# The head attentions of a vision tower leave the row statistics to the norms behind them

## The chip, the cores and the metric

One core of a Trainium2 chip runs the whole program. The time is that of one execution on the device, in microseconds; of several executions the median is given. Beside it there is one profiled execution, whose trace gives the start and length of each instruction.

## The reference

A small vision tower on 32 images of 50 tokens (49 patches and a class token), 192 features, float32. Four layers follow the patch embedding, each a mixer and a feed-forward part, each behind a layer norm and added to h. What matters here lies in layers 1 and 2:

```python
# layer 1's feed-forward part: a transformer block with experts, on x = layernorm(h)
#   LN(ln1) -> attention of 12 heads of 16 -> projection, added -> LN(ln2) -> 8 experts, top 2
h = h + _L1_ffn_ref(_layernorm(h), ...)
# layer 2's mixer: attention of 12 heads with q and k of length one
h = h + _L2_attn_ref(_layernorm(h), ...)
# layer 2's feed-forward part: 8 experts with a capacity, on the norm of what the mixer wrote
h = h + _L2_ffn_ref(_layernorm(h), ...)
```

A layer norm takes mean and variance over the 192 features of each token.

## The kernel before

The 1600 tokens lie as 16 tiles of 100 tokens (two images), a token to a partition, in h and x (100 x 16 x 192). Each stage is a block with one program for each engine; between two blocks there is a barrier of all engines. Semaphores order the engines within a block.

`heads_attention` (line 1378) is used twice: in layer 1 it adds to x, and GpSimd adds each finished tile of x to h (`join`, line 1428); in layer 2 it adds to h, and there is no join. Its loop runs over the tiles, two to a round of the hardware loop. In a step VectorE copies the transposed queries and keys of the next tile out of PSUM (`take_qkT`, lines 1646 and 1647), adds the output projection of the last tile to its row (`add`, 1662), takes the highest scores (1651), scales q and k into `wide` (1638, or 1633 in layer 2), multiplies by the inverse sums (1656), copies v (1642), and at the end of the step takes the statistics of the tile that it added (`count`, 1667, a bn_stats into t.bn). TensorE transposes q and k (1465), multiplies the scores (1479, 1487), weighs the values (1496), projects the output (1504) and makes the q, k, v of a later tile (1453, 1454). After the loop VectorE counts the last tile and turns the 16 sets of statistics into mean and variance in t.mv (bn_aggr, 1707).

`normalise` (line 286) is the norm in front of every part. It goes in four groups of four tiles. For a group `collect` takes the statistics (bn_stats 353, bn_aggr 356), unless `ready` says that t.mv holds them, and adds eps (366); ScalarE takes the root (408) behind a table load (403); `spread` takes the reciprocal (371). VectorE does collect(g) ahead of spread(g - 1). Then the rows are scaled (324), some by VectorE in spread, the others by GpSimd, which waits for a group's reciprocal. TensorE transposes each pair of tiles (453), and ScalarE copies them into xT (415, or 418 in two instructions with gain and bias). Who scales a tile is set by these lines:

```python
turn = [2 if ready or i >= TILES - GROUP else GROUP if y is None else TILES for i in range(TILES)]
by_vector = [i for i in range(TILES) if i % turn[i] == 0 and turn[i] < TILES]
```

The norm of layer 2's mixer (line 2150) comes behind experts, loads its h from memory and takes its own statistics. The norm of the last layer's experts (line 2543) does so too. Behind the norm of an expert part comes the router's block, with a table load (1118) and matmuls of the gate (1111).

Of the kernel before, what the change touches and what calls it, by code (L numbers as in the profile page):

```python
# [24 lines left out]
TILES = TOKENS // TILE  # L25
# [1127 lines left out]
def turn(t, src, dst):  # L1153

    nc = t.nc
    n = src.shape[2]
    turned = t.sem("turned")
    with t.block() as block:
        @block.tensor
        def _(pe):  # L1160
            for i in range(TILES):
                nc.tensor.transpose(t.bank[i // 4][0:n, TILE * (i % 4):TILE * (i % 4 + 1)], src[:, i, :],
                                    t.w["ident"][0:TILE, 0:TILE]).then_inc(turned, 1)

        @block.scalar
        def _(act):
            for c in range(CHUNKS):
                act.wait_ge(turned, 4 * c + 4)
                nc.scalar.activation(dst[:, CHUNK * c:CHUNK * (c + 1)], t.bank[c][0:n, 0:CHUNK], ACT.Identity)
# [208 lines left out]
def heads_attention(t, wqkv, proj, dst, unit, total=None):  # L1378
# [5 lines left out]
    nc, w = t.nc, t.w  # L1384
    GROUPS, DEEP = HEADS // 4, HEAD + 3
    with ExitStack() as st:
# [15 lines left out]
        (cleared, wproj_in, biased, staged, projected, values_up, squared, summed, logged, rooted, q_done, v_done,  # L1402
         turned, qkT_done, scored, max_done, shift_turned, shiftedT_done, scoredT, exp_done, weighed, sums_logged,
         inv_done, a_done, out_done, added, front_step) = (t.sem(n) for n in names)
        counted = t.sem("counted")
        bankQ, bankV, bankO, bankR, bankS = t.bank[0], t.bank[1], t.bank[2], t.bank[3], t.bank[4:8]
        wholeS = t.psum[0:TILE, 4 * 512:8 * 512].rearrange("p (j n) -> p j n", j=4)[:, :, 0:GROUPS * TILE]
        kT_at = slice(DIM, DIM + GROUPS * TILE)
# [1 line left out]
        with t.block() as block:  # L1410
# [194 lines left out]
            def _(dve):  # L1605
# [12 lines left out]
                def lengths(n):  # L1618
                    if unit:
                        dve.wait_ge(squared, n + 1)  # L1620
                        nc.vector.tensor_reduce(norm[:, 2, :], sq[:].rearrange("p (h e) -> p h e", e=HEAD),
                                                AX.X, ALU.add).then_inc(front_step, 1)
                        dve.wait_ge(front_step, 2 * n + 1)

                        nc.vector.tensor_scalar(norm[:, 0, :], norm[:, 2, :], 1e-24, None, ALU.max).then_inc(summed, 1)

                def take_qk(n, v):
                    if unit:
                        dve.wait_ge(rooted, n + 1)
                        nc.vector.tensor_tensor(norm[:, 1, 0:HEADS], norm[:, 1, 0:HEADS], w["L2_scale"][:],  # L1630
                                                ALU.mult).then_inc(front_step, 1)
                        dve.wait_ge(front_step, 2 * n + 2)
                        nc.vector.tensor_tensor(wide[:, v, :, 0:HEAD], narrow,
                                                norm[:, 1, :].unsqueeze(2).to_broadcast([TILE, 2 * HEADS, HEAD]),
                                                ALU.mult).then_inc(q_done, 1)
                    else:
                        dve.wait_ge(projected, n + 1)
                        nc.vector.tensor_scalar(wide[:, v, :, 0:HEAD], narrow, HEAD ** -0.25, None, ALU.mult).then_inc(q_done, 1)

                def take_v(n, v):  # L1640
                    dve.wait_ge(values_up, n + 1)
                    nc.vector.tensor_copy(v_[:, v, :, 0:HEAD], bankV[0:TILE, 0:DIM].rearrange("p (h e) -> p h e", e=HEAD)).then_inc(v_done, 1)

                def take_qkT(n):
                    dve.wait_ge(turned, n + 1)
                    nc.vector.tensor_copy(qkT[:, 0], bankQ[:, 0:GROUPS * TILE].rearrange("p (g n) -> p g n", g=GROUPS))
                    nc.vector.tensor_copy(qkT[:, 1], bankV[:, kT_at].rearrange("p (g n) -> p g n", g=GROUPS)).then_inc(qkT_done, 1)

                def highest(n, v):
                    dve.wait_ge(scored, n + 1)  # L1650
                    nc.vector.tensor_reduce(wide[:, v, 0:HEADS, HEAD + 2].rearrange("p (g j) -> p j g", j=4),
                                            wholeS.rearrange("p j (g n) -> p j g n", g=GROUPS), AX.X, ALU.max).then_inc(max_done, 1)

                def weighted(n):
                    dve.wait_ge(inv_done, n + 1)
                    nc.vector.tensor_tensor(aT[:].rearrange("p g n -> p (g n)"), bankO[:, 0:GROUPS * TILE],
                                            inv[:].rearrange("p g n -> p (g n)"), ALU.mult).then_inc(a_done, 1)

                def add(n):
                    dve.wait_ge(out_done, n + 1)  # L1660
                    tile = dst[:, bass.ds(n, 1), :]
                    nc.vector.tensor_tensor(tile, tile, bankO[0:TILE, 0:DIM].unsqueeze(1), ALU.add).then_inc(added, 1)

                def count(n):
                    dve.wait_ge(added, n + 1)
                    at = bass.ds(n, 1)
                    nc.vector.bn_stats(t.bn[:, at, :], dst[:, at, :]).then_inc(counted, 1)

                def step(n, u, first=False, final=False):
                    if not final:  # L1670
                        take_qkT(n + 1)
                    if not first:
                        add(n - 1)
                    if not final:
                        highest(n + 1, 1 - u)
                        if unit:
                            lengths(n + 2)
                            take_qk(n + 2, u)
                            weighted(n)
                        else:  # L1680
                            weighted(n)
                            take_qk(n + 2, u)
                        take_v(n + 2, u)
                    else:
                        weighted(n)
                    if not first:
                        count(n - 1)

                lengths(0)
                take_qk(0, 0)  # L1690
# [5 lines left out]
                take_v(1, 1)  # L1696
                dve.wait_ge(biased, 1)
                step(0, 0, first=True)
                with dve.Fori(0, TILES // 2 - 1) as i:
                    for u in range(2):  # L1700
                        step(2 * i + u + 1, 1 - u)
                step(TILES - 1, 1, final=True)
                add(TILES - 1)
                count(TILES - 1)
                for i in range(TILES):
                    dve.wait_ge(counted, i + 1)
                    nc.vector.bn_aggr(t.mv[:, i, :], t.bn[:, i, :])

BLOCK = 256
SUBS = BLOCK // 128  # L1710
# [414 lines left out]
def gates(t, w, rows):  # L2125
    return [w[0:rows, 0, :], w[0:HALF, 1, :]]


def xT_tile(t, rows):
    return lambda i, k: t.xT[0:rows if k == 0 else HALF, k, TILE * i:TILE * (i + 1)]  # L2130


def layer1_ffn(t):

    w = t.w
    normalise(t, t.h, 1e-5, keep=t.x, second=1e-5, gain=w["L1_ln1_g"], bias=w["L1_ln1_b"], ready=True)
    heads_attention(t, w["L1_qkv"], "L1_proj", t.x, unit=False, total=t.h)
    normalise(t, t.x, 1e-5, keep=t.x, gain=w["L1_ln2_g"], bias=w["L1_ln2_b"], ready=True)
    with ExitStack() as st:
        share = t.sbuf("share8", [TILE, TILES, 8], st)  # L2140
        shareT = t.sbuf("shareT", [8, 1, TOKENS], st)
        picked = [t.sbuf(f"pick{j}", [TILE, TILES, 8], st) for j in range(2)]
        route(t, xT_tile(t, HALF + 1), gates(t, w["L1_gate"], HALF + 1), 8, 2, masks=picked, weights=share)
        turn(t, share, shareT[:, 0, :])
        add_back(t, shareT, t.h, lambda g, i: w["L1_b2"][:, g, :])
        experts(t, "L1", t.x, t.h, picked, share, 8, ACT.Gelu, gated=False, norm=w["L1_ln2"])


def layer2_mixer(t):
    normalise(t, t.h, 1e-5, load=t.sums)  # L2150
    heads_attention(t, t.w["L2_qkv"], "L2_proj", t.h, unit=True)
# [6 lines left out]
def layer2_ffn(t):  # L2158


    nc, w = t.nc, t.w
    E, M = L2_EXPERTS, HIDDEN // 128
    size = [TILE, TILES, E]
    normalise(t, t.h, 1e-5, keep=t.x, ready=True)
    with ExitStack() as st:
        combine = t.sbuf("combine", [128, E // 2, TOKENS], st)
        taken = t.sbuf("taken", [HALF, 2, E, GROUPS2, SLOTS2], st)
# [383 lines left out]
def tower(nc, args, out, where):  # L2551
    with ExitStack() as stack:
        t = Tower(nc, stack, args, where)
        embed(t)
        zero_spare(t)
        layer0_mixer(t)
        layer0_ffn(t)
        layer1_mixer(t)
        layer1_ffn(t)
        layer2_mixer(t)  # L2560
        layer2_ffn(t)
        layer3_mixer(t)
        layer3_ffn(t, out)
# [190 lines left out]
```

## Time and profile before

| | |
|---|---|
| time, median of 3 executions | 2697.13 us (2692.56 to 2702.44) |
| time of the profiled execution | 2709.01 us |
| its span, first to last instruction | 2707.1 us |
| its mean granted TensorE clock | 0.847 |
| TensorE matmuls busy | 2114.3 us, 78% |
| VectorE busy | 1240.3 us, 46% |
| ScalarE busy | 858.6 us, 32% |
| GpSimd busy | 838.9 us, 31% |

The busy shares are means over stages with different limits. The span leaves out what lies around the first and last instruction (1.9 us here). The granted clock is given as a part of 2.4 GHz: 1.00 is that, 0.50 is 1.2 GHz. Layer 1's head attention and the norm behind it lie between about 647 and 798 us of the span, layer 2's between about 1052 and 1220 us.

### The profile page before, as it was taken

The page shows a single profiled execution, that of the slowest core. Times are in us where ns is not written, and L with a number is a line of the kernel's source. Part 1 is how long each engine was busy: PE and PEld are TensorE (multiplying, and loading weights), DVE is VectorE, ACT ScalarE, POOL GpSimd, SP SyncE. Part 2 cuts the span into 40 slices and gives each one's busy share as a digit, 9 for nine tenths or more (in the row PEclk, how much of TensorE's full clock was granted, in tenths as well). Part 3 has the DMA queues.
Part 4 walks back from the last instruction along what each step waited for, and adds up shares of the span by engine and source line. Part 5 has one row for each costly group of instructions (what it writes and reads, how often), then busy time and mean ns, then how long its engine had stood idle before and what let it go on. Part 6 is the DMA issues. An engine that isn't in the chain of part 4 may idle for free. (4 is left out here: it accounts for less than half of the span.)

```text
span 2707.1 us, 41933 instructions
## 1 busy us (share of the span) xinstructions
PE 2114.3 (78%) x13260; PEld 1508.9 (56%) x13260; DVE 1240.3 (46%) x2831; ACT 858.6 (32%) x1713; POOL 838.9 (31%) x788
## 2 busy tenths in 40 slices
PE   9746778886985894986899737777489944999998
PEld 9412224574763783654467312222479933999987
DVE  4249992323544113553113479998622236222222
ACT  1247862122332332342111545554112212111111
POOL 0204542203121553010001247665134421434443
PEclk9658996775876995997899769999689966999999
DMA  7000000000004761000210000000267614777774
GB/s 214 15 0 1 0 0 0 0 0 7 0 1 118 204 180 31 0 0 0 70 52 18 0 0 0 0 0 0 53 204 221 198 24 142 228 223 229 217 203 126
DMA packets 77951, 201.86 MB, mean 75 GB/s; under 512 B 17777, under 2 KB 47348, under 8 KB 69524
## 3 DMA queue, kind: packets, MB, share of 16 engines
q1 hardware_dynamic: 52820, 169.74, 19.6%
q0 software_dynamic: 25056, 31.22, 6.7%
q8 instruction: 35, 0.57, 0.1%
q14 instruction: 40, 0.33, 0.0%
HBM read 179.25 MB, written 22.91 MB: 75 GB/s over the span
## 5 line engine op out<-in xcount | busy, mean ns | idle before, releaser
L1858 POOL DMA_INDIRECT sums<-yblock,put x129 | 205.8, 1596 | 422.1 <-DVE yblock L2121 245.5
L1906 PE MATMUL banks<-xTblock,wt 128*128 128x256 f32 (+1 forms) x1464 | 268.0, 340 | 1.6 <-ACT xTblock L1977 1.2
L1931 PE MATMUL banks<-wt,hid 128*128 128x192 f32 x1548 | 267.2, 327 | 0.0
L2111 DVE TENSOR_TENSOR hid<-sa,banks 128x512 f32<-128x512 f32 (+1 forms) x183 | 105.8, 578 | 339.3 <-ACT sa L1998 336.4
L1931 PEld LDWEIGHTS banks<-wt,hid 128*128 128x128 f32 x1548 | 251.5, 191 | 0.1
L1906 PEld LDWEIGHTS banks<-xTblock,wt 128*128 128x128 f32 x1464 | 237.1, 194 | 23.5 <-issue 1.6
L1998 ACT ACTIVATE sa<-banks 128x512 f32<-128x512 f32 (+1 forms) x183 | 93.3, 510 | 481.6 <-PE banks L1917 476.6
L722 PE MATMUL banks<-g,consts 128*128 128x400 f32 x384 | 184.7, 571 | 60.2 <-DVE g L861 56.2
L830 POOL TENSOR_TENSOR w<-u,spreadB 128x400 f32<-128x400 f32 x192 | 192.7, 1033 | 87.2 <-ACT spreadB L801 87.2
L1853 POOL DMA_INDIRECT xblock<-table,take x135 | 135.0, 1000 | 223.3 <-DVE put L2087 175.3
L855 DVE TENSOR_TENSOR_SCAN s<-banks,w 128x400 f32<-128x400 f32 x192 | 188.9, 984 | 4.2 <-POOL w L830 4.2
L324 POOL TENSOR_SCALAR rows<-h,mv,sd 100x192 f32<-100x192 f32 x69 | 69.9, 1026 | 328.0 <-DVE sd L371 328.0
L722 PEld LDWEIGHTS banks<-g,consts 128*128 128x128 f32 x384 | 61.0, 197 | 168.5 <-DVE g L861 167.2
L613 POOL TENSOR_TENSOR w<-u,r 128x400 f32<-128x400 f32 x96 | 99.1, 1034 | 175.4 <-ACT r L587 162.9
L785 ACT ACTIVATE banks<-rate,coef 128x392 f32 x192 | 113.2, 591 | 117.8 <-DVE s L855 117.8
L2121 DVE TENSOR_SCALAR yblock<-banks,gate 128x192 f32<-128x192 f32 x129 | 49.4, 415 | 208.3 <-PE banks L1931 208.3
L1917 PE MATMUL banks<-xTblock,wt 64*128 64x256 f32 (+1 forms) x1464 | 143.2, 342 | 0.0
L1917 PEld LDWEIGHTS banks<-xTblock,wt 64*128 64x128 f32 x1464 | 116.0, 187 | 22.9 <-issue 11.9
L861 DVE TENSOR_TENSOR g<-s,banks 128x400 f32<-128x400 f32 x192 | 104.7, 547 | 0.0
L2304 PE MATMUL banks<-taken,wu 96*128 x192 | 86.3, 610 | 12.7 <-DMA wd<-L_down 10.0
L636 DVE TENSOR_TENSOR_SCAN s<-banks,w 128x400 f32<-128x400 f32 x96 | 94.3, 983 | 0.1
L453 PE MATMUL banks<-consts,rows 100*96 100x100 f32 (+1 forms) x192 | 44.3, 368 | 61.5 <-DVE rows L324 35.8
(416 smaller groups left out, 3743.5 us busy)
## 6 DMA issues: line engine op xcount, KB each, us to landing
wt<-L3f_packed SPq DMA_DIRECT2D x41, 1152.0 KB, 5.8
wt<-L3f_packed SPq DMA_DIRECT2D x41, 576.0 KB, 6.0
wt<-L3m_packed SPq DMA_DIRECT2D x20, 1152.0 KB, 5.7
wt<-L_packed SPq DMA_DIRECT2D x20, 579.0 KB, 4.4
wt<-L3m_packed SPq DMA_DIRECT2D x20, 577.0 KB, 5.9
wt<-L_packed SPq DMA_DIRECT2D x20, 576.0 KB, 4.2
pixels<-pixels SPq DMA_DIRECT2D x16, 375.0 KB, 5.0
wu<-L_up SPq DMA_DIRECT2D x8, 576.0 KB, 4.7
```

What stands on the lines that cost most here:

```text
L613: nc.gpsimd.tensor_tensor(w1[:, j % SLOTS, :], u[:, group(j), at], r[:, j % SLOTS, :], ALU.mult).then_inc(w1_done, 1)
L722: nc.tensor.matmul(acc[g][0:parts, 0:CHUNK], ident[0:parts, 0:parts], g_[:, j % SLOTS, :], start=(n == 0), stop=(n == STATES - 1)).then_in ...
L785: nc.scalar.activation(rest, rate[:, g, at].rearrange("p (b t) -> p b t", t=SEQ)[:, :, 1:SEQ], ACT.Exp, scale=coef[:, g, n:n + 1]).then_in ...
L830: nc.gpsimd.tensor_tensor(w2[:, j % SLOTS, :], u[:, g, at], spreadB[:, n % 2, :], ALU.mult).then_inc(bu_done, 1)
L855: nc.vector.tensor_tensor_scan(s[:, j % SLOTS, :], decays[j % DECAYS], w2[:, j % SLOTS, :], 0.0, ALU.mult, ALU.add).then_inc(s_done, 1)
L861: nc.vector.tensor_tensor(g_[:, j % SLOTS, :], s[:, j % SLOTS, :], bankC[(j // groups) % 2][0:parts, 0:CHUNK], ALU.mult).then_inc(g_done, 1)
L1853: nc.gpsimd.indirect_dma_start(x[:, b % 2, q - column_of_block[b], :], None, table, bass.IndirectOffsetOnAxis(take[:, q:q + 1], 0)).then_i ...
L1858: nc.gpsimd.indirect_dma_start(t.sums, bass.IndirectOffsetOnAxis(put[:, q:q + 1], 0), y[:, b % 2, q - column_of_block[b], :], None, comput ...
L1906: nc.tensor.matmul(bank[:, n * j:n * (j + 1)], wt[:, v, cols(base, 2 * p + j)], xT[:, v, 0, 0:n], start=(j == 0), stop=False, skip_group_c ...
L1917: last = nc.tensor.matmul(bank[:, n * j:n * (j + 1)], wt[half, v, cols(REST_AT, 2 * p + j)], xT[half, v, 1, 0:n], start=False, stop=True, ...
L1931: last = nc.tensor.matmul(bankY[s], hid[:, m, 128 * s:128 * (s + 1)], wt[:, v, DOWN_AT + DIM * m:DOWN_AT + DIM * (m + 1)], start=(m == 0 a ...
L2111: nc.vector.tensor_tensor(hid[:, 2 * p:2 * p + 2, 0:n], sa[:, (PAIRS * v + p) % 2, 0:2 * n].rearrange("p (m n) -> p m n", m=2), second[:, ...
```

## The change

The head attention no longer takes statistics of the rows that it writes, in the loop or behind it, and the semaphore `counted` goes. The two norms behind it (lines 2138 and 2164) are called without `ready`, so that they take bn_stats and bn_aggr in their own groups, and the list `turn` comes out as for the other norms without `ready`.

```diff
@@ heads_attention
-        counted = t.sem("counted")
...
-                def count(n):
-                    dve.wait_ge(added, n + 1)
-                    at = bass.ds(n, 1)
-                    nc.vector.bn_stats(t.bn[:, at, :], dst[:, at, :]).then_inc(counted, 1)
-
                 def step(n, u, first=False, final=False):
...
                     else:
                         weighted(n)
-                    if not first:
-                        count(n - 1)
...
                 step(TILES - 1, 1, final=True)
                 add(TILES - 1)
-                count(TILES - 1)
-                for i in range(TILES):
-                    dve.wait_ge(counted, i + 1)
-                    nc.vector.bn_aggr(t.mv[:, i, :], t.bn[:, i, :])
@@ layer1_ffn
-    normalise(t, t.x, 1e-5, keep=t.x, gain=w["L1_ln2_g"], bias=w["L1_ln2_b"], ready=True)
+    normalise(t, t.x, 1e-5, keep=t.x, gain=w["L1_ln2_g"], bias=w["L1_ln2_b"])
@@ layer2_ffn
-    normalise(t, t.h, 1e-5, keep=t.x, ready=True)
+    normalise(t, t.h, 1e-5, keep=t.x)
```

## Rows read from the trace of the kernel before

**Rows 1.** The page's first line: span and instructions.

```profile
span 2707.1 us, 41933 instructions
```

**Rows 2.** Timeline, layer 1's loop, high clock: start, us, engine, line, operation [idle before].

```profile
730.12 0.35 DVE L1667 BATCH_NORM_STATS2 bn<-x  x1
...
736.86 0.35 DVE L1667 BATCH_NORM_STATS2 bn<-x  x1
...
737.97 0.47 DVE L1646 COPY qkT<-banks 128x300 f32<-128x300 f32 x1 [0.76 <-PE banks L1465]
```

**Rows 3.** The removed line's own view: durations in ns, and who waited.

```profile
L1667 DVE BATCH_NORM_STATS2 bn<-x x16: 349/350/360, 687.6 to 783.8; - x14, 100x6 f32<-100x192 f32 x2
...
who waited for it (us, times):
busy tenths in 40 slices 0000000000000000000000000000000000000000
```

**Rows 4.** Timeline, layer 2's loop, high clock.

```profile
1192.05 0.35 DVE L1667 BATCH_NORM_STATS2 bn<-h  x1
...
1193.47 0.47 DVE L1646 COPY qkT<-banks 128x300 f32<-128x300 f32 x1 [1.07 <-PE banks L1465]
```

**Rows 5.** Timeline, layer 1's loop at the low clock.

```profile
674.93 0.36 DVE L1642 COPY v<-banks 100x192 f32<-100x192 f32 x1 [1.22 <-PE banks L1454]
...
687.33 0.36 DVE L1642 COPY v<-banks 100x192 f32<-100x192 f32 x1 [1.22 <-PE banks L1454]
...
689.79 0.47 DVE L1646 COPY qkT<-banks 128x300 f32<-128x300 f32 x1 [1.83 <-PE banks L1465]
```

**Rows 6.** Timeline, the seam from layer 1's attention to the router.

```profile
783.45 0.35 DVE L1662 TENSOR_TENSOR x<-x,banks 100x192 f32<-100x192 f32 x1 [1.04 <-PE banks L1504]
...
783.88 0.59 POOL L1428 TENSOR_TENSOR h<-h,x 100x192 f32<-100x192 f32 x1 [3.92 <-DVE x L1662]
784.12 1.15 DVE L1707 BATCH_NORM_AGGREGATE mv<-bn 100x2 f32<-100x6 f32 x16
...
785.57 0.24 DVE L366 TENSOR_SCALAR sd<-mv 100x4 f32<-100x4 f32 x2 [0.31 <-PEq L104]
...
787.35 8.39 POOL L324 TENSOR_SCALAR x<-x,mv,sd 100x192 f32<-100x192 f32 x8 [2.87 <-DVE sd L371]
...
797.59 1.28 ACT L1118 ACT_TABLE_LOAD   x1 [0.27 <-PEq L104]
```

**Rows 7.** Timeline, the seam from layer 2's attention to the router.

```profile
1206.45 0.35 DVE L1662 TENSOR_TENSOR h<-h,banks 100x192 f32<-100x192 f32 x1 [1.04 <-PE banks L1504]
...
1207.12 1.15 DVE L1707 BATCH_NORM_AGGREGATE mv<-bn 100x2 f32<-100x6 f32 x16
...
1208.57 0.24 DVE L366 TENSOR_SCALAR sd<-mv 100x4 f32<-100x4 f32 x2 [0.30 <-PEq L104]
...
1220.12 1.28 ACT L1118 ACT_TABLE_LOAD   x1 [0.27 <-PEq L104]
```

**Rows 8.** Timeline, the norms of lines 2150 and 2543, with their successors' first instructions.

```profile
1036.17 1.14 DVE L353 BATCH_NORM_STATS2 bn<-h 100x6 f32<-100x192 f32 x4 [15.39 <-DMA h<-sums]
...
1039.51 11.10 POOL L324 TENSOR_SCALAR rows<-h,mv,sd 100x192 f32<-100x192 f32 x11 [14.49 <-DVE sd L371]
...
1052.03 1.28 ACT L1561 ACT_TABLE_LOAD   x1 [0.27 <-PEq L104]
...
2195.03 1.14 DVE L353 BATCH_NORM_STATS2 bn<-h 100x6 f32<-100x192 f32 x4 [15.59 <-DMA h<-sums]
...
2211.28 1.28 ACT L1118 ACT_TABLE_LOAD   x1 [0.27 <-PEq L104]
```

**Rows 9.** Timeline of GpSimd, first instruction behind a block that GpSimd ended.

```profile
647.17 1.38 POOL L1418 MEMSET wide<- 100x1536 f32 x1 [0.29 <-POOLq L104]
```

**Rows 10.** Windows behind the seams: stretch, us, TensorE busy, granted clock, DMA share, GB/s.

```profile
784.00:866.00 82.00, 41.39 (x191) 0.50 0.26 73
1208.00:1248.00 40.00, 25.23 (x120) 0.50 0.00 1
1248.00:1300.00 52.00, 38.35 (x125) 0.89 0.00 0
```

## What the change does to the time: the prediction

> **What bounds the kernel here.** I read the page first, then the timeline of both attentions at either clock, then the line of the removed statistics for who waits for it, then the two seams from attention to norm, then a norm of this kernel that already takes its own statistics, and last the granted clock behind the seams. The profiled execution has a span of 2707.1 us [rows 1] and a time of 2709.01 us; the three other executions have a median of 2697.13 us (2692.56 to 2702.44), so the profiled one was 0.4% slower than that. No single engine bounds the whole: the program is a row of stages with a barrier between each two, and a microsecond counts in a stage only if it lies on what that stage ends with. So the change touches four stages: two attentions, two norms. A measurement of this kernel can tell about 0.3%, 8.1 us, from no change.
>
> Inside the attention loops the statistics are the last thing VectorE does in a tile. In the first attention at the high clock (2.4 GHz) they start at 730.12 and again at 736.86, so a tile takes 6.74 us; they end at 737.21, and the copy of qkT behind them starts at 737.97 after 0.76 us of idling, released by TensorE's transposes [rows 2]. In the second attention the idle time behind them is 1.07 us [rows 4]. At the low clock (1.2 GHz) a tile takes 687.33 - 674.93 = 12.40 us, and VectorE idles 1.83 us there [rows 5]. The list of those who wait for the statistics is empty: the line of the heading is followed at once by the next heading's line [rows 3].
>
> **The change, part by part.**
>
> *The statistics in the loops (32 of 0.35 us), price 0.* What hides them is the wait for TensorE that follows. Without them the copy of qkT waits 0.35 us longer for the same transposes, which go by score_turned and v_done and not by the statistics. What would be bought if that cover weren't there is 32 x 0.35 = 11.2 us; this is the bound from below for the term. I take 0, since the idle time behind them (0.76 us at the least) is more than the pitch of 0.35 us. Above nothing there is nothing: no wait is added in the loops, and GpSimd's order there is untouched.
>
> *The end of the attentions.* In the first one the last add ends at 783.45 + 0.35 = 783.80; then come the statistics of the last tile and the 16 aggregations, which end at 784.12 + 1.15 = 785.27, and VectorE starts the norm at 785.57, 0.30 later. With the tail gone, GpSimd's last addition of x to h is what ends the block: 783.88 + 0.59 = 784.47 [rows 6]. Another block that GpSimd ended was followed 0.29 later by its successor [rows 9], so the norm starts at 784.77: 0.80 us saved. In the second attention GpSimd has no such addition, the last add ends at 1206.45 + 0.35 = 1206.80, the norm can start 0.30 later at 1207.10 and not at 1208.57 [rows 7]: 1.47 us saved. The count of tile 14, in the last step, lies in a wait for TensorE too and saves nothing. Together -2.27 us, the surest term.
>
> *The norms themselves.* Dropping `ready=True` does two things. The first is plain: collect(g) now runs four bn_stats and four bn_aggr before the variance, and since collect(1) stands ahead of spread(0) on VectorE, GpSimd's first tile waits for two groups of statistics. The second stands in the list `turn`: with ready every second tile is VectorE's (8 and 8); without it, and without y, every fourth is, and every second only in the last four, so VectorE has tiles 0, 4, 8, 12, 14 and GpSimd the eleven others. GpSimd's tiles follow each other without a gap, 8.39 us for 8 [rows 6], and it is their pace that the transposes, ScalarE's copies and the end of the norm go by.
>
> The price of both is in the trace already, since the norm behind the first experts (line 2150) is this very form: no second, no y, keep apart, 5 and 11 tiles. Its first statistics start at 1036.17, GpSimd starts 3.34 us later at 1039.51 and takes 11.10 us for its eleven, and the next block starts at 1052.03: 15.86 us from the first statistics to the successor. A second norm of the form took 2211.28 - 2195.03 = 16.25 us, a little of it a wait for its loads [rows 8]. The norms that are changed took 797.59 - 785.57 = 12.02 us [rows 6] and 1220.12 - 1208.57 = 11.55 us [rows 7] from VectorE's first instruction to the successor. The second has the same tail behind GpSimd as the form of rows 8, so it costs 15.86 - 11.55 = +4.31. The first has gain and bias, so that its last pair is copied in two instructions: behind GpSimd's end at 787.35 + 8.39 = 795.74 it takes 1.85 us. So it comes to 3.34 + 11.10 + 1.85 = 16.29, less 12.02 = +4.27. The bounds: below, if GpSimd kept eight tiles, only the later start counts, 3.34 less (787.35 - 785.57 = 1.78) = +1.56 for each; above, 16.25 for the form of rows 8, 0.39 us more for each. I take +4.31 and +4.27, by the nearest row. Square roots are no new term: ScalarE's table load lies beside the statistics, while before it was what VectorE waited for. Nothing runs beside these blocks that would hide the eleven tiles: TensorE and ScalarE wait for each, and no DMA is issued in them.
>
> The Trainium skill, SBUF — State Buffer (Who interferes with whom), has a rule that speaks of this move: VectorE and GpSimd share a port pair, and one blocks the other while it holds it, but an instruction of VectorE with at most one SBUF input outside the two-port modes does not contend. bn_stats has one input, so by the page the moved statistics cost GpSimd nothing; were they blocked for GpSimd's time, up to twelve bn_stats of 0.35 us, 4.2 us, would come on top for each norm. The trace agrees with the page: eleven tiles with statistics beside them took 11.10 us, 1.01 us each, and eight without took 8.39 us, 1.05 us each [rows 6, 8].
>
> *What follows.* Routing and experts start behind a barrier and issue their own loads, so they are moved and not changed. One semaphore less in each attention is one clearing less on SyncE, off the path. The sum: -2.27 + 4.27 + 4.31 = **+6.3 us**. On the profiled time that is 2715.3 us, on the median of the runs 2697.13 + 6.3 = 2703.4 us, 0.23% more.
>
> **The clock.** Behind both seams TensorE's granted clock is 0.50 (1.2 GHz) already: 784 to 866, and 1208 to 1248 [rows 10]. It fell when the attention's matmuls ended, so a norm that is 4 us longer has none to lose. What can move is where it rises again, and in the stretch 1248 to 1300 it goes up and down, 0.89 in the mean: (1 - 0.89) / 0.50 = 0.22 of 52 us, 11.4 us, at the low level, in which a stage that TensorE bounds could give back half or lose as much again: 5.7 us. This is chance from execution to execution, and I take 0 for it; four executions of the kernel before lie between 2692.56 and 2709.01 us.
>
> **The rivals.**
>
> *A: the clock moves with the norms.* The norms' 4 us of sparse transposes make the rise of the clock come later at one or two places behind. For it: the clock rose only at 866 behind the first and at 1248 behind the second, after stretches where TensorE worked 41.39 of 82 and 25.23 of 40 us. Against it: these stages start behind barriers and do the same work in the same order. Price, one stretch as above: +5.7, which gives 2709.1 us. The Trainium skill, TensorE: Matmul & The Clock Gate (Part 1), says that the throttled level is the default and that activity lifts it; by that rule more quiet time can only hurt, and the rows show the low level on both sides of the seam, so it has nothing to hurt inside the norm.
>
> *B: the same phase works the other way*, and the stretch of 0.89 comes out at the high clock: 6.3 - 5.7 = +0.6, 2697.7 us. For and against as with A.
>
> *C, the other side: the statistics in the loop were not hidden.* If TensorE's transposes are themselves let go by something behind the bn_stats on VectorE, each tile becomes 0.35 us shorter, 11.2 us in all, and with 6.3 the sum is -4.9: 2692.2 us. It decides from 6.3 / 32 = 0.20 us a tile on. For it: only that VectorE has the statistics inside each tile's round. Against it: nobody waits for them, and 0.76 us or more of idling comes right behind [rows 2 to 5].
>
> *D: the split stays 8 and 8* (or GpSimd's pace isn't what ends the norm): 1.56 x 2 - 2.27 = +0.9, 2698.0 us. The code of `turn` and rows 8 speak against it.
>
> **The chances.** Forecast 0.72, A 0.12, B 0.08, C 0.05, D 0.03. The median of a few executions moves by some 4 us either way, so of the forecast's 0.72 about 0.24 lie above 8.1 us, and of A most: slower 0.36; faster needs C and luck: 0.03; within 0.3%: 0.61. The range of the likeliest case alone is 2699 to 2708. With A, B and D in it and that scatter it is 2695 to 2711, which leaves out C and the far end of A, under 2 in 10.
>
> **What the profile after would show.** The tile rounds unchanged, 6.74 us in the first attention at the high clock, with the idle time ahead of the qkT copy grown to about 1.1 us. The norms' first bn_stats 0.3 us behind GpSimd's last addition in the first seam and behind VectorE's last add in the second. GpSimd's scaling 11 tiles in each norm, starting 3.3 us behind the first statistics. 16.3 and 15.9 us from there to the router's block. Clock 0.50 through both norms. The prediction is wrong if a tile round shrinks (C), if the norms have 8 tiles on GpSimd (D), or if the stages behind them change their length at another clock (A, B).

## The result, and the profile after

| | kernel before | changed kernel |
|---|---|---|
| median of 22 executions each | 2700.31 us | 2709.65 us |
| ratio | | 1.0035, 95% interval 1.0019 to 1.005 |
| a second comparison, 12 executions of the changed one | 2701.65 us | 2708.36 us, 1.0027, 1.0009 to 1.0045 |
| span of the profiled execution | 2707.1 us | 2702.2 us |

The change makes the kernel slower, by 0.27 and 0.35% in the two comparisons. The forecast was 2703.4 us and 0.23% more. (One of the 22 executions of before, 2850 us, was disturbed, and the ratios leave it out.)

The profiled execution of the changed kernel is 4.9 us *shorter* than that of before. Whoever compares the two spans gets the wrong sign. The changed kernel's profile was already 3.75 us ahead when the first attention concerned began (643.42 against 647.17), before anything that was changed; what the stages behind that point add is in the table. The stages are cut at ScalarE's table loads, of which each begins a block: 403 begins a norm, 1561 (1560 in the changed kernel) a head attention, 1118 the router.

| stage, us | before | changed | changed, second profile |
|---|---|---|---|
| layer 1's attention | 138.36 | 132.31 | 137.64 |
| the norm behind it | 12.06 | 16.47 | 16.49 |
| layer 2's attention | 156.50 | 154.65 | 150.57 |
| the norm behind it | 11.59 | 15.98 | 16.04 |

The norms come out the same in both profiles; the attentions don't. They are read below at their tails and rounds, at one level of TensorE's clock. (Layer 2's attention is the least steady stage of all: 150.57 us here in the second profile of the change, and 164.77 in that of experiment 6, which has the attention of before.)

The first seam in the changed kernel, timeline of all engines, which answers to [rows 6]:

```profile
774.42 0.35 DVE L1661 TENSOR_TENSOR x<-x,banks 100x192 f32<-100x192 f32 x1 [1.31 <-PE banks L1503]
774.85 0.59 POOL L1427 TENSOR_TENSOR h<-h,x 100x192 f32<-100x192 f32 x1 [3.92 <-DVE x L1661]
775.73 1.28 ACT L403 ACT_TABLE_LOAD   x1 [3.13 <-PEq L104]
775.77 1.14 DVE L353 BATCH_NORM_STATS2 bn<-x 100x6 f32<-100x192 f32 x4 [1.00 <-PEq L104]
...
777.22 0.17 DVE L366 TENSOR_SCALAR sd<-mv 100x4 f32<-100x4 f32 x1
777.30 1.13 DVE L353 BATCH_NORM_STATS2 bn<-x 100x6 f32<-100x192 f32 x4
...
778.82 0.17 DVE L371 RECIPROCAL sd<-sd 100x4 f32<-100x4 f32 x1
...
779.10 11.26 POOL L324 TENSOR_SCALAR x<-x,mv,sd 100x192 f32<-100x192 f32 x11 [3.66 <-DVE sd L371]
...
792.20 1.28 ACT L1118 ACT_TABLE_LOAD   x1 [0.27 <-PEq L104]
```

The reader is to see two things. GpSimd's last addition ends at 775.44 and the norm's first statistics start 0.33 later; from the last add's end (774.77) it is 1.00 us, where it was 785.57 - 783.80 = 1.77. And the first reciprocal stands behind two groups of statistics, so that GpSimd starts 3.33 us into the norm (before: 1.78) with eleven tiles in 11.26 us (before: eight in 8.39).

The second seam, VectorE's timeline; behind it GpSimd's and ScalarE's of the same stretch:

```profile
1201.79 0.35 DVE L1661 TENSOR_TENSOR h<-h,banks 100x192 f32<-100x192 f32 x1 [1.31 <-PE banks L1503]
1202.47 1.14 DVE L353 BATCH_NORM_STATS2 bn<-h 100x6 f32<-100x192 f32 x4 [0.32 <-PEq L104]
```

```profile
1205.79 11.19 POOL L324 TENSOR_SCALAR x<-h,mv,sd 100x192 f32<-100x192 f32 x11 [27.09 <-DVE sd L371]
```

```profile
1202.43 1.28 ACT L403 ACT_TABLE_LOAD   x1 [2.45 <-PEq L104]
...
1218.41 1.28 ACT L1118 ACT_TABLE_LOAD   x1 [0.27 <-PEq L104]
```

Here nothing of GpSimd's stands in the seam, and the norm starts 0.33 us behind the last add's end at 1202.14; it was 1.77 [rows 7].

The two norms by engine, windows of the changed kernel and then of before (us, busy time of PE, PEld, DVE, ACT and POOL with their instructions, granted clock, DMA share, GB/s):

```profile
775.73:792.20 16.47, 8.13 (x32) 4.17 (x32) 8.40 (x45) 9.21 (x21) 11.26 (x11) 0.50 0.00 0
1202.43:1218.41 15.98, 8.12 (x32) 4.16 (x32) 8.36 (x45) 5.88 (x14) 11.19 (x11) 0.50 0.00 1
```

```profile
785.53:797.59 12.06, 7.45 (x32) 4.45 (x32) 4.27 (x16) 9.23 (x22) 8.39 (x8) 0.50 0.00 1
1208.53:1220.12 11.59, 7.45 (x32) 4.45 (x32) 4.18 (x16) 5.88 (x13) 8.35 (x8) 0.50 0.00 1
```

VectorE's work doubles, from 4.3 to 8.4 us, and is still well under the norm's length; GpSimd is the busiest engine in both norms of the changed kernel. Before it was so in layer 2's alone: in layer 1's ScalarE was busy 9.23 us (1.28 of it the table load) and GpSimd 8.39. The clock is 0.50 in all four.

The loop of layer 1, VectorE's timeline of the changed kernel, answers to [rows 2]:

```profile
700.58 0.36 DVE L1641 COPY v<-banks 100x192 f32<-100x192 f32 x1 [0.36 <-PE banks L1453]
701.96 0.47 DVE L1645 COPY qkT<-banks 128x300 f32<-128x300 f32 x1 [1.03 <-PE banks L1464]
...
708.71 0.47 DVE L1645 COPY qkT<-banks 128x300 f32<-128x300 f32 x1 [1.03 <-PE banks L1464]
```

A tile takes 708.71 - 701.96 = 6.75 us with the statistics gone, as it did with them. The idle time ahead of the copy went from 0.76 to 1.03 us: what was removed became waiting. In layer 2 it went from 1.07 to 1.34, with rounds of 7.98 us in both kernels.

The whole of layer 1's attention says the same, if profiles are paired in which the clock rose at the same point. The first row is the changed kernel's; the two behind it are of experiment 1, which keeps the statistics in the loop:

```profile
643.42 1.28 ACT L1560 ACT_TABLE_LOAD   x1 [6.61 <-PEq L104]
```

```profile
642.84 1.28 ACT L1561 ACT_TABLE_LOAD   x1 [6.64 <-PEq L104]
...
773.83 0.35 DVE L1662 TENSOR_TENSOR x<-x,banks 100x192 f32<-100x192 f32 x1 [1.04 <-PE banks L1504]
```

From this load to the last add's end it is 774.77 - 643.42 = 131.35 us without the statistics and 774.18 - 642.84 = 131.34 with them. Where the clock rose later it is 136.67 without (second profile of the change) and 136.63 with (783.80 - 647.17, the kernel before).

By these stages the change costs 4.41 + 4.39 in the norms less 0.77 + 1.44 in the tails: **+6.6 us**, 0.24%, inside both measured intervals.

### The profile page after: what moved, and what is told of

The parts are those of the page before. It is cut to its first block and busy times, and to the rows that moved or that the text cites. A ratio compares the mean times of both kernels' runs of the same rounds, so it can differ in the third digit from the quotient of the medians.

```text
span 2702.2 us, 41903 instructions
## 1 busy us (share of the span) xinstructions
PE 2104.1 (78%) x13260; PEld 1500.7 (56%) x13260; DVE 1237.1 (46%) x2825; ACT 857.5 (32%) x1713; POOL 844.0 (31%) x794
```

## The experiments

Whole times scatter from one execution to the next (2691 to 2711 us for the kernel before), by more than these edits are worth, so each is read first at its stages, and the ratio stands beside it where it was timed.

**1. The norms alone.** The attentions stay as before; the norms lose `ready`, and the statistics are taken twice.

```diff
-    normalise(t, t.x, 1e-5, keep=t.x, gain=w["L1_ln2_g"], bias=w["L1_ln2_b"], ready=True)
+    normalise(t, t.x, 1e-5, keep=t.x, gain=w["L1_ln2_g"], bias=w["L1_ln2_b"])
...
-    normalise(t, t.h, 1e-5, keep=t.x, ready=True)
+    normalise(t, t.h, 1e-5, keep=t.x)
```

> The attentions stay as before, statistics and aggregations included; only the two norms lose ready, so that they take the statistics a second time. My theory: the whole loss is in the norms, the gain in the tails of the attentions. So the two norms take 16.4 and 16.0 us from table load to table load, against 12.06 and 11.59 before, the tails stay at 1.77 us from the last add's end to the norm, and the sum is +8.8 us, about 2.2 more than the change has by its stages. Rival (the loss of the change is partly elsewhere, for example in the attentions' loops without statistics): this kernel would then be nearer to before than the change is, under +6 us.

Measured: norms of 16.48 and 15.97 us, tails unchanged (last add's end to the norm 1.76 us both times), so +8.8 by the stages; ratio 1.0046, interval 1.0027 to 1.0064, that is +12.4 us (7.3 to 17.3). The whole loss is there with the attentions untouched, and by the stages it is larger than the change's own +6.6, as it should be where the tails save nothing; the ratios alone can't tell the two apart, since their intervals overlap. The rival's "under +6" is outside the interval.

**2. Eight tiles each.** The changed kernel, but `turn` is 2 for these two norms.

```diff
-    turn = [2 if ready or i >= TILES - GROUP else GROUP if y is None else TILES for i in range(TILES)]
+    turn = [2 if ready or halves or i >= TILES - GROUP else GROUP if y is None else TILES for i in range(TILES)]
```

> The changed kernel, but in the two norms VectorE and GpSimd take eight tiles each, as with ready. My theory, in which GpSimd's eleven tiles are most of the loss and the later start the smaller part: GpSimd still starts 3.3 us behind the first statistics, and works 8.4 us; the norms take about 13.6 and 13.2 us in place of 16.4 and 16.0, and the whole is about 1 us slower than before. Rival (the statistics on VectorE set the pace of the norm, not GpSimd's share): the norms stay within 1 us of 16.4 and 16.0, since VectorE has three more tiles of 0.38 us beside its statistics.

Measured: norms of 14.12 and 13.71 us, 2.35 and 2.27 shorter than the changed kernel's; ratio 1.0015 (0.9994 to 1.0037), stages +2.06 + 2.12 - 2.21 = +2.0 us. So just over half of the norms' loss was the split (2.35 of 4.41 and 2.27 of 4.39). They are 0.5 us longer than I expected, and GpSimd's timeline shows why:

```profile
787.15 2.09 POOL L324 TENSOR_SCALAR x<-x,mv,sd 100x192 f32<-100x192 f32 x2 [3.65 <-DVE sd L371]
789.57 2.10 POOL L324 TENSOR_SCALAR x<-x,mv,sd 100x192 f32<-100x192 f32 x2 [0.32 <-DVE sd L371]
791.99 4.07 POOL L324 TENSOR_SCALAR x<-x,mv,sd 100x192 f32<-100x192 f32 x4 [0.32 <-DVE sd L371]
```

With two tiles of a group GpSimd is done before VectorE has the next reciprocal, and it idles 0.32 us twice. The rival is right in that small part: at eight tiles each, VectorE's statistics begin to set the pace.

**3. Scale at once.** The changed kernel, but VectorE does spread(g) right behind collect(g) in these two norms.

```diff
                 for g in range(GROUPS):
                     collect(g)
-                    if g:
+                    if at_once:
+                        spread(g)
+                    elif g:
                         spread(g - 1)
-                spread(GROUPS - 1)
+                if not at_once:
+                    spread(GROUPS - 1)
```

> The changed kernel, but VectorE scales a group and releases it to GpSimd right after that group's own statistics, not after the next group's. My theory (the start is late because two groups of statistics lie ahead of the first reciprocal): GpSimd starts about 2.1 us behind the first statistics in place of 3.3, and each norm is 1.1 to 1.2 us shorter, 15.3 and 14.8 us. Rival (VectorE's wait for ScalarE's root in each group makes VectorE late for later groups, and GpSimd runs dry): gaps between GpSimd's tiles, and the norms no shorter than 16.4 and 16.0.

Measured: norms of 15.08 and 14.66 us, 1.39 and 1.32 shorter. VectorE's timeline, then GpSimd's:

```profile
784.89 1.14 DVE L353 BATCH_NORM_STATS2 bn<-x 100x6 f32<-100x192 f32 x4 [1.00 <-PEq L104]
...
786.78 0.18 DVE L371 RECIPROCAL sd<-sd 100x4 f32<-100x4 f32 x1 [0.27 <-ACT sd L411]
```

```profile
787.06 11.02 POOL L324 TENSOR_SCALAR x<-x,mv,sd 100x192 f32<-100x192 f32 x11 [2.51 <-DVE sd L371]
```

GpSimd starts 2.17 us into the norm and not 3.33, and has no gap in its eleven tiles. The wait for the root costs VectorE 0.27 us there and GpSimd nothing. So the later start is the other part of the loss, as far as it comes from the second group's statistics: 1.16 us of start, and 0.24 in GpSimd's own time (11.02 against 11.26), which I had not expected. This order and the split of experiment 2 were not run together. The whole time of its one execution says nothing at this size.

**4. Four counts.** The kernel before, with each tile's statistics taken four times.

```diff
+        scratch = t.sbuf("scratch", [TILE, 3, 1, 6], st)
...
                     nc.vector.bn_stats(t.bn[:, at, :], dst[:, at, :]).then_inc(counted, 1)
+                    for k in range(3):
+                        nc.vector.bn_stats(scratch[:, k], dst[:, at, :])
```

> The kernel before, but each tile's statistics are taken four times in the attention loops (three go to a scratch tile that nobody reads). It asks how much cover there is. My theory (hidden behind the wait for TensorE's transposes: 0.76 us idle in layer 1, 1.07 in layer 2): three more of 0.27 to 0.35 us take 0.8 to 1.05 us, so a round in layer 1 goes from 6.745 to between 6.75 and 7.05 us and in layer 2 it stays at 7.98. Rival C of the prediction (the statistics are in the tile's round in full): 7.6 to 7.8 us and 8.8 to 9.0 us.

Measured, VectorE's timeline in layer 1 and then in layer 2:

```profile
717.72 0.47 DVE L1647 COPY qkT<-banks 128x300 f32<-128x300 f32 x1
...
723.63 0.86 DVE L1670 BATCH_NORM_STATS2 scratch<-x 100x6 f32 x3
724.47 0.47 DVE L1647 COPY qkT<-banks 128x300 f32<-128x300 f32 x1
...
1172.72 0.47 DVE L1647 COPY qkT<-banks 128x300 f32<-128x300 f32 x1 [0.29 <-PE banks L1466]
...
1180.71 0.47 DVE L1647 COPY qkT<-banks 128x300 f32<-128x300 f32 x1 [0.29 <-PE banks L1466]
```

Rounds of 6.75 and 7.99 us. Three more bn_stats take 0.78 us of VectorE's time (1.07 - 0.29 in layer 2), and the rounds don't grow. In layer 1 the cover is used to its end: no idle time is left ahead of the copy. Rival C is refuted from the costly side, as it was from the cheap one by the changed kernel's own rounds. (The last tile's three stand behind the last add, where nothing covers them: from there to the norm it is 2.54 us in layer 1, 0.77 more than before.)

**5. Early aggregations.** The kernel before, with 14 of the 16 bn_aggr in the last step, behind add(14).

```diff
+                    if final:
+                        aggregate(range(n - 1))
...
                 count(TILES - 1)
-                for i in range(TILES):
-                    dve.wait_ge(counted, i + 1)
-                    nc.vector.bn_aggr(t.mv[:, i, :], t.bn[:, i, :])
+                aggregate((TILES - 2, TILES - 1))
```

> The kernel before with its statistics in the loop, but 14 of the 16 aggregations stand in the last step, ahead of the wait for the last tile's inverse sums, and only two stay behind the last add. My theory (a tail can be had for nothing without moving the statistics): the aggregations lie in idle time of VectorE, the last add ends as before, and the norm starts about 0.95 us behind it in place of 1.77 in both attentions; in layer 1 GpSimd's last addition to h ends first or at the same time. The norms keep 12.06 and 11.59 us. Sum -1.6 us. Rival: the aggregations push the last tile's work and the seam gains nothing.

Measured, the second seam, VectorE's timeline:

```profile
1190.43 0.35 DVE L1662 TENSOR_TENSOR h<-h,banks 100x192 f32<-100x192 f32 x1 [1.56 <-PE banks L1504]
1190.70 1.03 DVE L1672 BATCH_NORM_AGGREGATE mv<-bn 100x2 f32<-100x6 f32 x14
1193.16 0.47 DVE L1656 TENSOR_TENSOR aT<-banks,inv 128x300 f32<-128x300 f32 x1 [1.43 <-ACT inv L1589]
...
1194.94 0.35 DVE L1662 TENSOR_TENSOR h<-h,banks 100x192 f32<-100x192 f32 x1 [1.05 <-PE banks L1504]
...
1195.61 0.30 DVE L1672 BATCH_NORM_AGGREGATE mv<-bn 100x2 f32<-100x6 f32 x2
1196.21 0.24 DVE L366 TENSOR_SCALAR sd<-mv 100x4 f32<-100x4 f32 x2 [0.30 <-PEq L104]
```

The fourteen aggregations lie in VectorE's wait for the inverse sums, and the norm starts 0.92 us behind the last add's end at 1195.29 in place of 1.77; in the first seam 1.00. That is -0.85 and -0.77, with norms of 11.88 and 11.55 us, 0.18 and 0.04 less than before. In layer 1 this is all that the change won at this seam. There GpSimd's addition to h sets the end either way (here at 775.39), so the 0.95 us that I expected in both seams could not be reached.

**6. Three tiles of four on VectorE.** The kernel before, with another split in the two norms.

```diff
-    by_vector = [i for i in range(TILES) if i % turn[i] == 0 and turn[i] < TILES]
+    by_vector = [i for i in range(TILES) if (i % GROUP < 3 if most else i % turn[i] == 0 and turn[i] < TILES)]
```

> The kernel before, but in the two norms VectorE scales three tiles of four and GpSimd one. It tests the same cause from the other side: if GpSimd's share is what a norm's length goes by, fewer tiles on it must shorten the norm until VectorE or ScalarE takes over. My theory: GpSimd works about 4.2 us, layer 1's norm is then set by ScalarE's sixteen copies of 0.46 us and takes 10 to 11 us in place of 12.06, layer 2's by VectorE and takes 8.5 to 9.5 us in place of 11.59; the sum is -3 to -5 us. Rival (the port that VectorE and GpSimd share, or the barrier and table load, set the length): less than 1 us each.

Measured: norms of 10.16 and 8.66 us in place of 12.06 and 11.59, -4.8 us in all; ratio 0.9984 (0.9965 to 1.0003). GpSimd's timeline in the second norm, then ScalarE's of the same stretch:

```profile
1206.10 5.07 POOL L324 TENSOR_SCALAR x<-h,mv,sd 100x192 f32<-100x192 f32 x4 [27.00 <-DVE sd L371]
```

```profile
1204.28 1.28 ACT L403 ACT_TABLE_LOAD   x1 [3.90 <-PEq L104]
...
1212.17 0.50 ACT L415 ACTIVATE xT<-banks 96x400 f32<-96x400 f32 x1 [0.17 <-PE banks L453]
1212.94 1.28 ACT L1118 ACT_TABLE_LOAD   x1 [0.27 <-PEq L104]
```

GpSimd ends at 1211.17 and no longer sets the end: the next block starts 1.77 us later, where before it was 1.42 (1220.12 less 1218.70), and the copies follow each other with 0.16 to 0.17 us between them. The norm's length goes by who has the tiles, in both directions.

**7 and 9. Both.** Early aggregations and three of four together, timed twice.

> Both of the edits before together: early aggregations and three tiles of four on VectorE. The sum of the two, -5 to -6 us by the stages, if they don't share a wait; in the whole time about 0.2% under the kernel before, which is at the edge of what five rounds can tell.

> Early aggregations and three tiles of four on VectorE, once more, on the same chip as the changed kernel. By its stages it is 6.8 us faster than the kernel before, a ratio of 0.9975; the first time gave 0.9986 (0.997 to 1.0002). My theory: 0.996 to 0.999, and the two together tell it from 1. Rival (what the stages win is given back elsewhere): 1.000 or above.

Measured: 0.9986 (0.997 to 1.0002) and 0.9975 (0.9959 to 0.9991). In the first profile the norms take 10.14 and 8.39 us, in the second 10.17 and 8.66. By the stages that is (12.06 - 10.14) + (11.59 - 8.39) = 5.1 and 4.8 us in the norms, and 1.6 in the tails each time: from the last add's end to the norm's table load it is 0.96 or 0.97 us in layer 1 and 0.88 or 0.89 in layer 2, in place of 1.73. (VectorE's own first instruction in layer 2's norm comes later, at 1.31 us, and the norm's length holds that.) The sum is 6.7 and 6.4 us, where -5 to -6 was expected first and 6.8 then. The second comparison alone has its interval below 1; the first doesn't tell this version from before. The two weighed together give 0.998, give or take 0.001 (an estimate from the two intervals). On the same chip as the second the changed kernel had 1.0027 against the same executions of before, so that this version was faster than the change by about 0.5%.

**8. The change again.**

> The changed kernel once more, unedited. By its stages the change costs 6.6 us (two norms +4.41 and +4.39, two tails -0.77 and -1.44), by the whole time 9.4 us with an interval of 5.1 to 13.5. My theory: the 3 us between them are scatter of the clock's rises in other stages, so this time the ratio lies near 1.0024, between 1.0005 and 1.0045, and the stages of the seams come out as before to 0.1 us. Rival A of the prediction (the clock systematically rises later behind the longer norms): 1.0035 or more again.

Measured: ratio 1.0027 (1.0009 to 1.0045), norms of 16.49 and 16.04 us, tails of 1.00 and 0.32 us. The ratio that the stages give, 1.0024, lies in both intervals. A systematic loss behind the norms (rival A) isn't refuted by this, since 1.0035 lies in the interval too. What speaks for and against it stands under "What stays open".

## Why the prediction was right, point by point

| step | forecast, us | measured, us |
|---|---|---|
| statistics out of the loops | 0 (bound -11.2) | 0: rounds 6.74 and 6.75, with four counts 6.75; layer 1's whole attention 131.35 and 131.34 |
| tail of layer 1's attention | -0.80 | -0.77 |
| tail of layer 2's attention | -1.47 | -1.44 |
| norm of layer 1 | +4.27 | +4.41 |
| norm of layer 2 | +4.31 | +4.39 |
| sum | +6.3 | +6.6 |
| whole time | +6.3 (0.23%) | +9.4 and +7.3 by the ratios (0.35 and 0.27%) |

*The loops.* That VectorE's idle time grows by what is taken away was right: 0.76 to 1.03 us. It grew by 0.27, about the distance from one bn_stats' start to the next (0.78 / 3 = 0.26 in experiment 4), and not by its 0.35; I had named "about 1.1". So rival C's bound was drawn a little wide, 32 x 0.27 = 8.6 us.

*The tails.* The seam between two blocks, 0.29 to 0.30 us behind whoever ends last, was read from [rows 6, 7, 9] and came out at 0.33. That GpSimd ends the block in layer 1 and VectorE in layer 2 was right.

*The norms.* The term that carried the forecast was not built up from instructions but taken from another norm of the same form in the same trace [rows 8]: GpSimd's start 3.34 us in (3.33 and 3.32 measured) and 11.10 us of work (11.26 and 11.19). The 0.14 us by which layer 1's norm was forecast too short is this 0.16. Experiments 2 and 3 split it: at layer 1, 2.35 us of the 4.41 go with three tiles and 1.39 with the order of collect and spread. The other 0.67 no run takes by itself; GpSimd's start, which in experiment 3 is still 2.17 us in and not 1.78, has 0.39 of it.

*Table load.* It was no new term: the first root starts 0.41 us behind its end, since VectorE's variance comes later.

*The rivals.* D is refuted by the eleven tiles in the trace, C by the rounds and by layer 1's whole attention. D's price was too low: with eight tiles each the norms came out 2.06 and 2.12 us longer in experiment 2 and not 1.56, because GpSimd waited twice for VectorE there. A and B, the clock, are no part of the stages that make up the sum, and such scatter was there, so they belonged in the range; whether A adds anything of its own is open. What I had missed is where the clock would show: inside the attentions, ahead of the changed norms. Windows over layer 1's, of before and of the changed kernel (us, TensorE busy, granted clock, DMA share, GB/s):

```profile
647.00:691.50 44.50, 38.51 (x317) 0.50 0.03 10
691.50:783.80 92.30, 89.21 (x1596) 1.00 0.00 0
```

```profile
643.00:676.00 33.00, 26.76 (x210) 0.50 0.04 13
676.00:774.80 98.80, 95.64 (x1710) 1.00 0.00 0
```

The attention of the changed kernel spent 33 us at the low clock, that of before 44.5. With a tile at 12.40 us at the low clock and 6.74 at the high one [rows 5, 2], 11.5 us fewer are worth 11.5 x (1 - 6.74 / 12.40) = 5.2 us, and the stage is 6.05 shorter, of which 0.77 is the tail: 5.3 us. It isn't the change's doing: the second profile of the changed kernel has this stage at 137.64 us, and the kernel of experiment 5, whose loop still takes the statistics, at 132.34. I had placed the scatter in the stretch from 1248 to 1300 and priced it at 5.7 us. For layer 1's attention this was the right size; for layer 2's, 14 us apart between two profiles with granted clocks of 0.91 and 0.82 in the mean, it was far too little.

*What stays open.* The timed comparisons of the change and of experiments 1 and 2 lie 1 to 4 us above the sums of their stages, that of experiment 6 and the first of "both" 0.5 and 3 us above theirs, and the second of "both" 0.3 below. The intervals (some 4 us either way) hold the sums, but nearly all on one side is a hint that the later stages may lose a little. That would be rival A. The stretches behind the norms neither show it nor rule it out: from the router's load behind layer 1's norm to the next norm it is 234.3 us in the mean of the five profiles with longer norms and 232.7 in that of the six others, and the single ones lie between 229.8 and 236.0. The larger part of this, the experts' stage (from the load on line 1986 or its counterpart), ran from 164.2 to 170.6 us, in no order that goes with the edits. So the sum of +6.6 us is shown; the 1 to 3 us by which the ratios lie above it may be chance or A.

## What to carry to other kernels

Before work is taken off an engine in a loop, look at what ends its idle time right behind: if it waits there for another engine, the work was free, and moving it to a place that is a chain of short steps makes it cost something. A flag that says "this is done already" may also choose the split of work between engines; here that second effect was more than half of the loss. And where a trace holds another instance of the very form that a change brings about, take the whole duration of it, from barrier to barrier: it has the waits in it that a sum of instructions leaves out.

## What the runs showed of the hardware

GpSimd's time for a tile of 100 x 192 depended on what VectorE did beside it. With nothing beside it a tile took 1.00 to 1.01 us, and in experiment 3 one took 1.01 with bn_stats beside it all through. In experiment 6, where VectorE ran three scalings of 0.36 us in a row beside each of GpSimd's tiles, they took 1.19 to 1.20 us each; the 5.07 us of its row for four tiles hold two waits of 0.14 us as well. So bn_stats cost GpSimd nothing here, and the cost that the prediction weighed for it is there, if small, beside tensor_scalar. The Trainium skill, SBUF — State Buffer (Who interferes with whom), says that tensor_scalar can run in a two-port mode and then contends with GpSimd for a shared port pair. The slower pace agrees in direction; that this is its cause was not tested.

TensorE's clock rose 44.5 us into the same attention in one execution and 33 us into it in another, with TensorE busy 38.5 and 26.8 us before the rise. The difference in this one stage, 5.3 us, is nearly as large as the whole effect that was studied. Together with the 3.75 us that were gained before the changed stages began, it more than makes up for the loss in the two profiled spans.
